# First feed-forward of a four-layer gated transformer on one Trainium2 core: inputs in three bf16 planes, and the steps after the convolution in another order

## The reference

```python
def act_quant(x):
    scale = 127.0 / clip(max(abs(x), axis=-1), 1e-05)
    return clip(round(x * scale), -128, 127) / scale
def weight_quant(w):
    scale = 1.0 / clip(mean(abs(w)), 1e-05)
    return clip(round(w * scale), -1, 1) / scale
h = einsum('bsd,hd->bsh', act_quant(xn), weight_quant(w1))   # 256 -> 1024
h = depthwise_conv1d(h, conv_w, conv_b)                      # 3 taps along the 1024 rows
h = silu(h)
y = einsum('bsd,hd->bsh', act_quant(h), weight_quant(w2))    # 1024 -> 256
x = x + tanh(g_ffn[0]) * y
```

## Time and profile before

| what | us |
|---|---|
| median of three runs | 1902.67 |
| profiled execution, its own time | 1903.29 |
| its span, first to last instruction | 1901.5 |
| TensorE matmuls busy | 1641.6 (86%) |
| VectorE busy | 1162.2 (61%) |
| ScalarE busy | 882.7 (46%) |
| GpSimd busy | 321.7 (17%) |
| L372, the up matmuls, busy | 126.1, 256 records |

### The profile page before, as it was taken

The page is one execution under the profiler, slowest core; times in us unless marked ns, Lnnn a source line. Parts: engine busy times, 40 slices in busy tenths (PEclk is TensorE's granted clock), DMA queues, the critical chain, the costliest instruction groups (busy, mean ns, idle before and its releaser), DMA issues. The chain is left out here.

```text
span 1901.5 us, 29604 instructions
## 1 busy us (share of the span) xinstructions
PE 1641.6 (86%) x10149; PEld 1246.9 (66%) x10149; DVE 1162.2 (61%) x2598; ACT 882.7 (46%) x1795; POOL 321.7 (17%) x359
## 2 busy tenths in 40 slices
PE   7797788887899898799997489999945999989998
PEld 5453345556667666688885279999934888864446
DVE  4668577766456667888986823322247989862116
ACT  2332577664432221466553355555544565533213
POOL 0000000000000101111100345555552111101110
PEclk9898899998899999999998689999977999989999
DMA  6000000003000000100004912222253000000002
GB/s 201 1 1 1 1 1 1 1 1 127 1 1 1 1 1 1 31 2 1 2 1 155 333 59 70 73 71 73 71 191 89 1 1 2 1 1 0 0 1 89
DMA packets 62849, 78.83 MB, mean 41 GB/s; under 512 B 13179, under 2 KB 52655, under 8 KB 62319
## 3 DMA queue, kind: packets, MB, share of 16 engines
q1 hardware_dynamic: 43927, 48.14, 7.5%
q0 software_dynamic: 7584, 20.72, 3.5%
q10 hardware_dynamic: 11192, 8.06, 1.3%
HBM read 58.16 MB, written 18.74 MB: 40 GB/s over the span
## 5 line engine op out<-in xcount | busy, mean ns | idle before, releaser
L2994 PEld LDWEIGHTS moe_bank<-moe_xt,moe_w1e 128*128 128x128 f32 x1264 | 155.0, 193 | 5.8 <-DVE moe_xt L2842 1.8
L2994 PE MATMUL moe_bank<-moe_xt,moe_w1e 128*128 128x128 f32 x1264 | 155.8, 277 | 1.1 <-DVE moe_xt L2842 1.1
L3004 PE MATMUL moe_bank<-moe_w,moe_xin 128*128 x632 | 149.3, 379 | 0.0
L3068 ACT ACTIVATE moe_xin<-moe_bank,moe_b 128x128 f32<-128x128 f32 x316 | 90.3, 368 | 125.1 <-PE moe_bank L2994 125.0
L372 PE MATMUL l0f_hb<-l0f_xt,f_w 128*128 128x512 f32 x256 | 126.1, 625 | 5.3 <-DVE l0f_a L306 3.8
L1471 POOL TENSOR_TENSOR all_x<-all_x,l1x_fbias 128x256 f32<-128x256 f32 x32 | 23.3, 732 | 594.2 <-DVE l1x_fxn L204 594.2
L3004 PEld LDWEIGHTS moe_bank<-moe_w,moe_xin 128*128 128x128 f32 x632 | 114.0, 190 | 12.3
L209 DVE BATCH_NORM_STATS2 all_stats<-all_x 128x6 f32<-128x256 f32 x256 | 104.0, 421 | 5.2
L2851 DVE TENSOR_TENSOR moe_y<-moe_bank,moe_b2r 128x256 f32<-128x256 f32 x79 | 33.5, 424 | 118.8 <-PE moe_bank L3004 118.8
L2911 POOL DMA_INDIRECT moe_results<-moe_y,moe_row x79 | 78.0, 988 | 125.2 <-DVE moe_y L2851 121.9
L2842 DVE COPY moe_xt<-moe_bank 128x256 f32<-128x256 f32 x79 | 33.5, 425 | 106.7 <-PE moe_bank L2982 106.7
(11 more groups left out here) (484 smaller groups left out, 3807.5 us busy)
## 6 DMA issues: line engine op xcount, KB each, us to landing
moe_w<-in_L_ffn_W SPq DMA_DIRECT2D x32, 512.0 KB, 10.4
moe_w<-moe_results SPq DMA_DIRECT2D x16, 512.0 KB, 8.8
all_x<-in_x SPq DMA_DIRECT2D x4, 1024.0 KB, 12.5
out_x<-all_x SPq DMA_DIRECT2D x8, 512.0 KB
f_w<-in_L_ffn_w_T SPq DMA_DIRECT2D x2, 1024.0 KB, 13.7
moe_inputs<-moe_xin ACTq DMA_DIRECT2D x8, 256.0 KB, 7.5
moe_inputs<-moe_w1e ACTq DMA_DIRECT2D x8, 256.0 KB, 7.8
moe_b2r<-in_L_ffn_b SPq DMA_DIRECT2D x1, 2048.0 KB, 14.2
```

Source lines behind the costliest of these rows:

```text
L2994: ins = nc.tensor.matmul(out, w1e[:, at:at + P], xt[:, u, c * P:(c + 1) * P], start=(c == 0), stop=(c == DC - 1))
L3004: ins = nc.tensor.matmul(bank[4 + u][:, 0:D], ht[:, u, c * P:(c + 1) * P], w2[:, ds(e * (HC * D) + c * D, D)], start=(c == 0), stop=(c == ...
L3068: ins = nc.scalar.activation(ht[:, u, m * P:(m + 1) * P], bank[1 + u][:, m * P:(m + 1) * P], ACT.Gelu, bias=b1[:, ds(e * HC + m, 1)])
```

## The change

- The input of the up matmuls is held as three bf16 tensors ("planes") that add up to the f32 value: the first is x rounded to bf16, the second the rest rounded to bf16, the third what is then left. The rounded w1, which is -1, 0 or 1, is written as bf16 too. So `up` does two times three bf16 matmuls per half instead of two f32 ones.
- The planes of the first batch are made ahead of the loop: ScalarE copies each pair twice from PSUM (bf16 plane and f32 rows), VectorE subtracts (`rest`), ScalarE copies the rest to bf16 (`middle`), VectorE subtracts again (`low`). VectorE's norm scales come behind this.
- The planes of the other batches are made by GpSimd: per pair of tiles two copies to bf16 and two subtractions, each waiting for the one ahead. `xt` is now single; the planes are double-buffered by batch. `up(g, 0)` waits for the first four tiles of its batch, `up(g, 1)` for all eight.
- `zq` is double-buffered; turn_back, copy_q and down work on tile t-2 in step g (update and stats on t-3). `largest_hidden(t-1)` leads VectorE's step, quantise(t-1) follows on ScalarE, and silu is done for slot g-2.
- TensorE's step is turn_back(t-2, first half), up(g, first half), turn_back(t-2, second half), up(g, second half), turn_x, down(t-2), turn_z(t); for t > TAIL the last two change places.
- ScalarE's step is centre(g-1), silu(g-2), quantise_x, copy_q(t-2, first half), quantise(t-1) of both halves, copy_q(t-2, second half), norm, copy_x; for t > TAIL both copy_q stand ahead of quantise.

```diff
-        w1, w2, w2q, wscale, wmean = f.w1, f.w2, f.w2q, f.wscale, f.wmean
+        w1, w2, w2q, wscale, wmean = f.w1b, f.w2, f.w2q, f.wscale, f.wmean
-        xt = s.sb("xt", [P, 2, DC, S])
+        xt = s.sb("xt", [P, DC, S])
+        xs = s.sb("xs", [P, 2, 3, DC, S], BF16)
-        zq = s.sb("zq", [P, 2, HM * P])
+        zq = s.sb("zq", [P, 2, 2, HM * P])
...
             @block.vector
+                def rest(t):
+                    dve.wait_ge(s.xt_ready, t + 2)
+                    nc.vector.tensor_tensor(rows(t), rows(t), plane(t, 0), ALU.subtract).then_inc(s.rest_ready, 2)
+                def low(t):
+                    dve.wait_ge(s.mid_ready, t + 2)
+                    nc.vector.tensor_tensor(plane(t, 2), rows(t), plane(t, 1), ALU.subtract).then_inc(s.xs_ready, 2)
                 for t in range(TB):
                     dequantise(t)
+                for t in range(0, TB + 2, 2):
+                    if t < TB:
+                        rest(t)
+                    if t >= 2:
+                        low(t - 2)
                 norm_range(nc, c, sh, TB, T)
...
-                for g in range(END + 3):
+                for g in range(END + 4):
-                    if 0 <= t - 2 < T:
-                        update(t - 2)
+                    if 0 <= t - 1 < T:
+                        largest_hidden(t - 1)
+                    if 0 <= t - 3 < T:
+                        update(t - 3)
                     if 1 <= g <= SLOTS:
                         conv(g - 1, 0)
                         conv(g - 1, 1)
...
-                    if 0 <= t < T:
-                        largest_hidden(t)
...
+            @block.gpsimd
+            def _(pool):
+                k = Chain(pool, s.split_step)
+                for t in range(TB, T, 2):
+                    pool.wait_ge(s.xt_ready, t + 2)
+                    if t % TB == 0 and t >= 2 * TB:
+                        pool.wait_ge(s.h_ps, (t // TB - 1) * M)
+                    k.link(nc.gpsimd.tensor_copy(plane(t, 0), rows(t)))
+                    k.link(nc.gpsimd.tensor_tensor(rows(t), rows(t), plane(t, 0), ALU.subtract))
+                    k.link(nc.gpsimd.tensor_copy(plane(t, 1), rows(t)))
+                    nc.gpsimd.tensor_tensor(plane(t, 2), rows(t), plane(t, 1), ALU.subtract).then_inc(s.xs_ready, 2)
...
             @block.tensor
+                    pe.wait_ge(s.xs_ready, b * TB + (half + 1) * TB // 2)
                     if half == 0:
-                        pe.wait_ge(s.xt_ready, (b + 1) * TB)
                         if g >= 2:
                             pe.wait_ge(s.conv_ready, g - 1)
                     for d in range(DC):
-                        ins = nc.tensor.matmul(hb[g % 2][:, half * 512:(half + 1) * 512], w1[:, d, m * P:(m + 1) * P],
-                                               xt[:, b % 2, d, half * 512:(half + 1) * 512], start=(d == 0), stop=(d == DC - 1))
+                        for k in range(3):
+                            ins = nc.tensor.matmul(hb[g % 2][:, half * 512:(half + 1) * 512], w1[:, d, m * P:(m + 1) * P],
+                                                   xs[:, b % 2, k, d, half * 512:(half + 1) * 512],
+                                                   start=(d == 0 and k == 0), stop=(d == DC - 1 and k == 2))
...
             @block.scalar
                 def copy_x(t):
                     act.wait_ge(s.xt_ps, t + 2)
...
+                    if t < TB:
+                        nc.scalar.activation(pair(plane(t, 0)), turned(t), ACT.Copy)
+                    else:
+                        act.wait_ge(s.xs_ready, t - TB + 2)
+                    nc.scalar.activation(pair(rows(t)), turned(t), ACT.Copy).then_inc(s.xt_ready, 2)
+                def middle(t):
+                    act.wait_ge(s.rest_ready, t + 2)
+                    nc.scalar.activation(plane(t, 1), rows(t), ACT.Copy).then_inc(s.mid_ready, 2)
...
                 def quantise(t, half):
                     act.wait_ge(s.sc2_ready, t + 1)
-                    if t:
-                        act.wait_ge(s.back_ps, 2 * (t - 1) + half + 1)
+                    if t >= 2:
+                        act.wait_ge(s.back_ps, 2 * (t - 2) + half + 1)
```

More of the change, by code:

```diff
@@ L248, in stage_l0_ffn, with rows, plane @@
         tg = sh.gates[:, 4:5]
+        def rows(t):
+            j = t % TB
+            return xt[:, :, j * P:(j + 2) * P]
+        def plane(t, k):
+            b, j = t // TB, t % TB
+            return xs[:, b % 2, k, :, j * P:(j + 2) * P]
         def z_bank(t):
@@ L419, in _ @@
                 fed = TB
-                for g in range(END + 2):
+                for g in range(END + 3):
                     t = g - LAG
                     b, m = g // M, g % M
[L423 to L427, removed]
+                    if 0 <= t - 2 < T:
+                        turn_back(t - 2, 0, fed)
                     if g < SLOTS:
                         up(g, 0)
[L430 to L434, removed]
+                    if 0 <= t - 2 < T:
+                        turn_back(t - 2, 1, fed)
                     if g < SLOTS:
@@ L437, in _ @@
                     if b < B - 1 and m >= HM:
-                        turn_x(fed, max(0, 2 * t))
+                        turn_x(fed, max(0, 2 * (t - 1)))
                         fed += 2
-                    if 0 <= t - 1 < T:
-                        down(t - 1)
+                    if 0 <= t - 2 < T and t <= TAIL:
+                        down(t - 2)
+                    if 0 <= t < T:
+                        turn_z(t, 0)
+                        turn_z(t, 1)
+                    if t > TAIL and t - 2 < T:
+                        down(t - 2)
             @block.scalar
@@ L494, in _ @@
                     quantise_x(t)
-                for t in range(0, TB, 2):
-                    copy_x(t)
+                for t in range(0, TB + 2, 2):
+                    if t < TB:
+                        copy_x(t)
+                    if t >= 2:
+                        middle(t - 2)
                 act.wait_ge(s.small_loaded, 32)
@@ L500, in _ @@
                 nc.scalar.activation(w2[:, :, :], w2[:, :, :], ACT.Copy, bias=MAGIC, scale=wscale[:, 1:2]).then_inc(s.w2_scaled, 1)
-                for g in range(END + 2):
+                for g in range(END + 3):
                     t = g - LAG
                     b, m = g // M, g % M
+                    if 1 <= g <= SLOTS:
+                        centre(g - 1)
+                    if 2 <= g <= SLOTS + 1:
+                        silu(g - 2)
                     if b < B - 1 and m >= HM:
@@ L506, in _ @@
                         quantise_x((b + 1) * TB + 2 * (m - HM) + 1)
-                    if 1 <= g <= SLOTS:
-                        centre(g - 1)
+                    if 0 <= t - 2 < T:
+                        copy_q(t - 2, 0)
+                        if t > TAIL:
+                            copy_q(t - 2, 1)
                     if 0 <= t - 1 < T:
-                        copy_q(t - 1, 0)
-                        copy_q(t - 1, 1)
+                        quantise(t - 1, 0)
+                        quantise(t - 1, 1)
+                    if 0 <= t - 2 < T and t <= TAIL:
+                        copy_q(t - 2, 1)
                     if b < B - 1 and m < HM:
@@ L514, in _ @@
                         norm((b + 1) * TB + 2 * m + 1)
-                    if 1 <= g <= SLOTS:
-                        silu(g - 1)
-                    if 0 <= t < T:
-                        quantise(t, 0)
-                        quantise(t, 1)
                     if b < B - 1 and m >= HM:
```

22 lines of the change are left out of this document (11 added, 11 removed).

## The result

The changed kernel took 1878.29 us (median of four runs, 1876.24 to 1881.22) beside 1902.81 for the kernel before on the same chip: ratio 0.9873, 95% interval 0.9857 to 0.9889. The forecast was 1878, the range 1872 to 1894. The profiled execution took 1877.65 (span 1875.9, before 1901.5).

The account below looks back on a forecast made before the run. Loops through ScalarE and VectorE, not TensorE, were taken to bound the first feed-forward. Opening, head, body and tail summed to a stage end of 426.2 against 451.17, -25.0 us from 1903.29: forecast 1878, range 1872 to 1894.

Parts of the forecast that it names:

- What bounds it: First feed-forward: loops through ScalarE and VectorE bind, not TensorE; 28 us less TensorE work alone is worth nothing.
- The loops: Steps between largest_hidden starts: 5.5 us last batch, 5.7 for m<4, 6.5 for m=3, 7.75 for m>=4.
- Ups: Up matmuls on TensorE: 0.214 us per bf16 matmul of 512 columns, 2.57 a slot against 3.44.
- GpSimd's pair: Planes of a tile pair on GpSimd: 4.0 us, covered except at a batch's first slot, about 0.6 delay there.
- Opening: Stage start to first centre: first-batch planes and later norm scales put the first centre at 199.0 against 195.63, +3.4 us.
- Head: Slots 0 to 8, before any tiles: last pair's planes at 238.8, first largest_hidden at 244.8.
- clock in the head (+2): One of the forecast's own bounds: TensorE's clock in the head could add 2 us.
- Body: From largest_hidden of tile 0 to that of tile 24: 152.6 us, to 397.4.
- Tail: Last eight tiles: 2.73 us apart against 3.62, 26.3 us in all, plus 2.5 for TensorE's clock.
- the first (GpSimd): Rival: GpSimd's pairs are slow (7.1 us) or the port holds dequantise; 1900, at 6 us 1884, likely 1888; chance 0.14.
- The second: Rival: TensorE's clock falls in the body, at 0.88 adding 7 to 13 us, 1885 to 1891; chance 0.12.
- third: Rival: TensorE stays at 1.2 GHz through the body, slots 10 to 31; 1910 us or more; chance 0.04.

Follow-up runs that it names:

- planes_alone: The kernel before with the bf16 planes and GpSimd's block, its old order kept: 1901.24 us, ratio 0.9994.
- deq_first: The changed kernel with dequantise moved ahead of the two taps in VectorE's step: 1865.87 us, ratio 0.98.
- order_alone: The changed kernel's new order with f32 up matmuls as before, no planes and no GpSimd work: 1876.62 us, ratio 0.9862.
- clock_fill: The changed kernel with twelve unread bf16 matmuls in each of the two steps behind the last ups: one run of 1881.81 us.
- pool_longer: The changed kernel with five more casts of the same plane in GpSimd's work on each pair of tiles: one run of 1898.6 us.
- order_deq: order_alone with the edit of deq_first: 1866.37 us, ratio 0.9803.

## Why the prediction was right, and where it wasn't

- **What bounds it, and that cheaper ups are worth nothing in the old loop**: right. planes_alone keeps 6.55 and 8.35.
- **The loops**: 5.5, 5.7, 6.5 and 7.75 were forecast; 5.49, 5.6, 6.36 and 7.70 came. They were added up start to start from rows of the kernel before, and each link is in the rows of after. deq_first shows that the link through dequantise was the one that held the m >= 4 steps.
- **Ups**: 0.214 each was twice the row of 256 columns; 0.215 came. What the prediction overlooked is what room the ups have to leave: "TensorE is not the bound" holds for the old order alone. In the new one f32 ups bind at 6.06 (order_alone), so that the planes do earn 3.7 us in the body. There the prediction left a part of the gain without a price.
- **GpSimd's pair**: forecast 4.0, measured 3.82 (237.46 to 241.28); no dequantise was held in the body, in the head it took 0.66 instead of 0.61.
- **Opening**: +3.4 forecast, +3.2 came (the four terms behind the fourth pair add up to 193.9, not 194.1, which changes nothing); the same from order_alone, whose first tap is 16.2 after the start against 19.6.
- **Head**: the step that failed. The centre of slot 8 was forecast 59.8 after the stage's start and came at 61.7, the first LH was forecast at 64.3 and came at 66.8. The pair's planes were only 0.6 late. The rest is clock, a term that the sum had in its bounds ("clock in the head (+2)") and not in its value: from the end of the pair to centre 8 it took 2.8 us instead of 1.5, six ups at 0.43 instead of 0.215, and from there to LH, behind twelve more ups, 5.1 instead of 4.5. It isn't there in every execution: clock_fill's, with the same head and a wait of the same length, takes 1.5 and 4.5 and has the first LH at 64.8.
- **Body**: 152.6 forecast, 154.1 measured. The loops of the body alone would give 151.6: the two steps without ups took 6.75 and 6.70, 2.5 more than 5.49 twice. The forecast had these 2.5 as a clock term but booked them behind tile 24, one stretch too late. (Its other reading of this place holds: in the kernel before the clock came back as the last tiles loaded TensorE, 0.68 in 420 to 424 and 1.00 in 424 to 428, though the rows 1 that it names stop at 421.5.)
- **Tail**: 2.73 forecast, 2.74 measured; 26.3 without the clock term booked there, 26.9 measured.
- **Rivals**: the first (GpSimd) priced each us of a pair at one us per boundary. By pool_longer it is 1.5 to 1.7 (5.1 to 5.9 for 3.4), while the held dequantise costs 0.13 a step and not 1.4. Both sizes were wrong, and they partly cancelled: a pair of 7.1 was priced at 22 us more, one of 7.2 cost 16.8 in the stage. (That the run of 1898.6 is so near the 1900 owes 4.2 to the time outside the stage.) The second and third (the clock falls in the body) didn't come in the changed kernel's profile: 1.00 throughout the body, with gaps of 0.62 and 1.05 in most steps with m >= 4. The second isn't empty, though: in clock_fill's execution the clock fell once in the same code and cost 1.7 us. Beside the second stood the Trainium skill, TensorE: Matmul & The Clock Gate, "A second HAM failure mode: psum-queue depth-cycling", that short idle spells can make the clock go up and down. The profile of the change doesn't show that in the body; clock_fill's shows one fall, and no going up and down.
- **The total**: the profiled execution is 25.6 shorter than that of before because -22.8 in the stage met -2.8 outside it, which is noise. Inside the stage the misses cancel in part as well: head +2.5, body +1.5, tail -1.9, and the clock is in all three.

## What to carry to other kernels

Work out the loop through all engines before pricing a cheaper instruction: TensorE's ups became 25% cheaper and that alone gave nothing, while moving whole steps gave 26.6 us of stage and moving three lines another 13.6 with the planes (1.3 of it by a clock that didn't fall) and 9.5 without them. Where an engine waits (2.22 us) for a chain that starts with its own late instruction, put that instruction first. And ask again after each change of order who is the bound: the planes cost up to 3.8 us, then nothing, and then earned 4.6, as the order around them got better and as the engine that was in the way was relieved of making them.

## What the runs showed of the hardware

- Two dequantise of 128x256 take 0.61 us beside no GpSimd instruction in the body. Where they start 0.40 into a GpSimd subtraction of 1.16 (deq_first, body) they take 1.17: the first one ends 0.15 after the subtraction and takes 0.90 instead of 0.34. They take 0.66 in the head of the changed kernel, 0.73 in the body and 1.11 to 1.37 in the head of pool_longer, and 1.51 to 1.57 in the head of deq_first, against 0.75 in order_deq's head, where GpSimd has no work. That fits a tensor_scalar that is held until the running GpSimd instruction ends and isn't held for the whole chain of four.
- A stop of TensorE of 4.07 us cost 1.7 us more in clock. One of 3.3 cost about 2 in one execution and nothing in another, and one of 1.95 cost 1.7 in one and nothing in another. The gaps of 0.62 and 1.05 in most steps with m >= 4 went with a clock of 1.00.
- Three bf16 matmuls of 512 columns (0.65) take three quarters of one pair of f32 records (0.86).
